# A graph network's edge passes: the right hand side table moves from device memory into on-chip memory

## The reference, cut to what matters

```python
def _gatv2(x, src, dst, edge_attr, Wl, bl, Wr, br, We, att, bo):
    xl = x @ Wl.T + bl
    xr = x @ Wr.T + br
    e = edge_attr @ We.T
    m = xl[src] + xr[dst] + e
    score = jnp.where(m > 0, m, NEG_SLOPE * m) @ att
    smax = jax.ops.segment_max(score, dst, num_segments=N)
    es = jnp.exp(score - smax[dst])
    denom = jax.ops.segment_sum(es, dst, num_segments=N)
    alpha = es / (denom[dst] + 1e-16)
    out = jax.ops.segment_sum(alpha[:, None] * xl[src], dst, num_segments=N)
    return out + bo
h = relu(_gatv2(x, src, dst, edge_attr, Wl1, ...)); h = _instance_norm(h)
h2 = relu(_gatv2(h, src, dst, edge_attr, Wl2, ...) + x @ Wskip.T + bskip)
```

## Time and profile before

| | us |
|---|---|
| median of three timed runs | 7746.43 |
| the profiled execution's own time | 7695.61 |
| its span | 7693.8 |
| PE busy | 5787.1 |
| DVE busy | 4073.2 |
| POOL busy | 3044.5 |
| ACT busy | 2576.5 |

### The profile page before, as it was taken

The page is one execution under the profiler, slowest core; times in us unless marked ns, Lnnn a source line. Parts: engine busy times, 40 slices in busy tenths (PEclk is TensorE's granted clock), DMA queues, the critical chain, the costliest instruction groups (busy, mean ns, idle before and its releaser), DMA issues. The chain is left out here.

```text
span 7693.8 us, 170283 instructions
## 1 busy us (share of the span) xinstructions
PE 5787.1 (75%) x40448; PEld 4192.9 (54%) x40449; DVE 4073.2 (53%) x12741; ACT 2576.5 (33%) x4844; POOL 3044.5 (40%) x3157
## 2 busy tenths in 40 slices
PE   4776777777777776577777777777777697999699
PEld 3555555555555555455555555555555583222689
DVE  6454555555555555455555555554555527778532
ACT  2233333333333333333323333332333215777210
POOL 3455555555555553455555555555555000000000
PEclk9888888888888888788888888888888898999899
DMA  3332322232232222332223323322222372323479
GB/s 78 74 77 67 78 77 71 77 79 69 76 77 68 77 72 60 77 79 69 76 69 78 78 69 77 77 71 77 77 70 77 149 274 78 133 104 109 172 296 362
DMA packets 689322, 764.62 MB, mean 99 GB/s; under 512 B 368995, under 2 KB 574026, under 8 KB 664145
## 3 DMA queue, kind: packets, MB, share of 16 engines
q1 hardware_dynamic: 561703, 577.65, 24.3%
q0 software_dynamic: 100352, 102.96, 6.9%
q10 hardware_dynamic: 27180, 82.93, 2.8%
HBM read 671.04 MB, written 88.81 MB: 99 GB/s over the span
## 5 line engine op out<-in xcount | busy, mean ns | idle before, releaser
L336 POOL DMA_INDIRECT gat_rows<-rows_scr,gat_idx x3136 | 3017.7, 962 | 2881.3 <-PE gat_aps L1352 1261.8
L1343 PE MATMUL gat_tps<-ident,gat_weights 128*128 128x128 f32 x3136 | 602.2, 323 | 1356.4 <-ACTq L1208 1237.9
L1343 PEld LDWEIGHTS gat_tps<-ident,gat_weights 128*128 128x128 f32 x3136 | 384.7, 159 | 1544.8 <-ACTq L1208 1372.0
L1225 ACT ACTIVATE adj_tiles<-gat_counts 128x392 f32 (+1 forms) x784 | 390.6, 498 | 2206.4 <-remote 1153.7
L1361 PE MATMUL gat_sps<-gat_relu,gat_att 128*128 128x256 f32 x3136 | 1084.7, 479 | 0.0
L1124 DVE CUSTOM_DVE_ANT_0 gat_masked<-gat_sps,gat_miss,gat_oldtop 128x512 f32<-128x512 f32 x784 | 586.6, 748 | 782.2 <-remote 513.0
L1075 DVE TENSOR_SCALAR adj_hot_key<-adj_iota_key,adj_winbase,adj_key 128x392 bf16<-128x392 int16 x2416 | 962.1, 398 | 7.6 <-issue 7.6
L1352 PE MATMUL gat_aps<-gat_rows,gat_weightsT 128*128 128x65 f32 x6224 | 957.9, 307 | 0.0
L1352 PEld LDWEIGHTS gat_aps<-gat_rows,gat_weightsT 128*128 128x128 f32 x6224 | 940.8, 231 | 0.0
L1116 DVE COPY gat_oldtop<-gat_top 128x1 f32 x784 | 119.8, 153 | 1354.8 <-issue 610.3
L1074 DVE TENSOR_SCALAR adj_hot_lo<-adj_iota_lo,adj_low 128x128 bf16<-128x128 int16 x2416 | 631.8, 261 | 265.3 <-issue 110.8
(11 more groups left out here) (384 smaller groups left out, 6824.3 us busy)
## 6 DMA issues: line engine op xcount, KB each, us to landing
gcn_sum_adj<-adj_scr SPq DMA_DIRECT2D x98, 1568.0 KB, 8.4
gat_dstb<-dst_scr SPq DMA_DIRECT2D x784, 128.0 KB
gat_ea<-in_ea SPq DMA_DIRECT2D x784, 128.0 KB
gin_sum_adj<-adj_scr SPq DMA_DIRECT2D x49, 1568.0 KB, 8.4
adj_scr<-adj_tiles ACTq DMA_DIRECT2D x48, 1568.0 KB
at_adj<-adj_scr SPq DMA_DIRECT2D x60, 1024.0 KB, 9.5
gat_rows<-rows_scr,gat_idx POOLq DMA_INDIRECT x3136
gat_xr<-xr_scr SPq DMA_DIRECT2D x1568, 24.0 KB
```

Source lines behind the costliest of these rows:

```text
L336: pool.indirect_dma_start(ring.rows[:, u, c, 0:ROW], None, rows_d, bass.IndirectOffsetOnAxis(ap=ring.idx[:, u, c:c + 1], axis=0)).then_inc ...
L1343: last = pe.transpose(tps[:, c * P:(c + 1) * P], wts[:, j, c * P:(c + 1) * P], ident[:])
```

## The change

The table of xr gets a buffer of its own on chip (`plan.right`), with a zeroed column block behind it for the empty row. It is no longer stored. In each visit DVE copies the two halves (64 partitions by 192 columns each) into a small buffer of four slots, from which PE reads as before. The source indices ride as four more 32-bit words at the end of each partition's 256 attribute words, so that one load brings both. To make room, the prologue's search uses other buffers' memory, and the weights and masked scores lie in a node table that is free during the passes; in pass 2 DVE therefore waits until ACT's six copies of the table are done before it clears one of them.

```diff
+RECORD = GE // 2 + GC
...
-def first_indices(sp, tag, words, ring, src_d):
+def first_edges(sp, tag, words, ring, edges_d):
...
-        sp.dma_start(ring.idx[:, u, :], src_d[bass.ds(group_of(sp, pair, group, u), 1), :, :]).then_inc(ring.s_first, 16)
+        sp.dma_start(ring.edges[:, u, :], edges_d[bass.ds(group_of(sp, pair, group, u), 1), :, :]).then_inc(ring.s_first, 16)
...
 def right_table(plan):
-    return plan.tiles[:].rearrange("p s h w d -> p (s h w d)")[:, 0:NT * XR].rearrange("p (t f) -> p t f", f=XR)
+    return plan.right[:, 0:NT, :]
...
-            act.wait_ge(s_part, 6)
-            act.wait_ge(s_clear, 1)
-            store_right(act, xr_d, xr3, empty_row, s_xr_out, [(0, NT)])
             act.wait_ge(s_skip_row, 1)
...
-        xr = sb("xr", [P, RING, XR], BF16)
+        xr = sb("xr", [P, 4, XR], BF16)
...
             def group_parts(u, first=False):
                 g = group_of(sp, pair, group, u)
                 if not first:
-                    sp.dma_start(idx[:, u, :], src_d[bass.ds(g, 1), :, :]).then_inc(s_id[u], 16)
+                    sp.dma_start(edges[:, u, :], edges_d[bass.ds(g, 1), :, :]).then_inc(s_id[u], 16)
                 sp.dma_start(dstb[:, u, :], dst16_d[bass.ds(g, 1), :].to_broadcast([P, GE])).then_inc(s_id[u], 16)
-                sp.dma_start(ea[:, u, :], ea_d[bass.ds(g, 1), :, :]).then_inc(s_ld[u], 16)
-
-            def range_parts(u):
...
-                for j in range(2):
-                    sp.dma_start(xr[HALF * j:HALF * (j + 1), u, :],
-                                 xr_d[bass.ds(blocks[j], 1), :, :]).then_inc(s_ld[u], 16)
...
-            if second:
-                sp.wait_ge(s_clear, 1)
-                store_right(sp, xr_d, xr3, empty_row, s_xr_out, PARTS, s_part)
-                sp.wait_ge(s_xr_out, 80)
-                for u in range(RING):
-                    load_pair(0, u)
-                    range_parts(u)
...
             dve.memset(relu[:, 1, :], 0.0)
+            if second:
+                dve.wait_ge(s_part, 6)
             dve.memset(wtsT[:, 1, :], 0.0)
...
+                    dve.reg_add(blocks[0], fresh[u], 1)
+                    dve.reg_alu(blocks[0], blocks[0], 1, ALU.logical_shift_right)
+                    dve.reg_alu(blocks[1], fresh[u], 1, ALU.logical_shift_right)
+
                     dve.wait_ge(s["top"], count("top", step, 3))
                     dve.wait_ge(s_loaded, step + 1)
                     dve.nop(nofuse=True)
                     dve.tensor_copy(top[:, bass.ds(tb, 1)], newtop[:, (u - 3) % 2:(u - 3) % 2 + 1]).then_inc(s["topped"], 1)
+                    for j in range(2):
+                        part = slice(HALF * j, HALF * (j + 1))
+                        of = dve.snap(blocks[j], min_val=0, max_val=NT)
+                        dve.tensor_copy(xr[part, u % 4, :], plan.right[part, bass.ds(of, 1), :].rearrange("p a f -> p (a f)"))
                     dve.tensor_scalar(hit[:, u % 4, :], near, node, None, ALU.is_equal)
...
-                    pe.wait_ge(s_ld[v], filled * 48 + 48)
                     pe.wait_ge(s_g[v], filled * (16 * GC) + 16 * GC)
                     pe.nop(nofuse=True)
-                    pe.matmul(mps[j][:, 0:GE // 2], we[:], ea[:, v, :], start=True, stop=False)
+                    pe.matmul(mps[j][:, 0:GE // 2], we[:], edges[:, v, 0:GE // 2], start=True, stop=False)
```

More of the change, by code:

```diff
@@ L195, in linear @@
 @phase
-def linear(nc, k, tag, h, w_d, width, out, ident, ring=None, rows_d=None, src_d=None, code_d=None):
+def linear(nc, k, tag, h, w_d, width, out, ident, ring=None, rows_d=None, edges_d=None, code_d=None):
     s_w, s_one = k.sem(tag + "_w"), k.sem(tag + "_one")
@@ L288, in __init__ @@
         self.tiles = sb("tiles", [P, 2, NT, WT, WD], BF16)
+        self.right = sb("right", [P, NT + 1, XR], BF16)
 class Ring:
@@ L371, in prologue @@
     s_skip_w, s_skip_row, s_skip_evac = k.sem("pro_skip_w"), k.sem("pro_skip_row"), k.sem("pro_skip_evacuated")
-    s_part, s_rest, s_xr_out, s_clear = (k.sem("pro_" + n) for n in ("part", "rest", "xr_stored", "empty_row"))
+    s_part, s_rest = (k.sem("pro_" + n) for n in ("part", "rest"))
     xr3, rest = right_table(plan), square
@@ L783, in window_search @@
         def window_search(dve, a):
-            dve.tensor_scalar(junk[:], ranges[:, 1, 0:NCH], wlo[:, a:a + 1], None, ALU.is_ge)
+            dve.tensor_scalar(junk, ranges[:, 1, 0:NCH], wlo[:, a:a + 1], None, ALU.is_ge)
             dve.drain()
-            dve.scalar_tensor_tensor(cond[:], ranges[:, 0, 0:NCH], whi[:, a:a + 1], junk[:], ALU.is_le, ALU.mult)
+            dve.scalar_tensor_tensor(cond, ranges[:, 0, 0:NCH], whi[:, a:a + 1], junk, ALU.is_le, ALU.mult)
             dve.drain()
-            dve.tensor_tensor_reduce(junk[:], cond[:], down[:], 1.0, 0.0, ALU.mult, ALU.max, accum_out=first[:, a:a + 1])
+            dve.tensor_tensor_reduce(junk, cond, down[:], 1.0, 0.0, ALU.mult, ALU.max, accum_out=first[:, a:a + 1])
             dve.drain()
-            dve.tensor_tensor_reduce(junk[:], cond[:], up[:], 1.0, 0.0, ALU.mult, ALU.max, accum_out=last[:, a:a + 1])
+            dve.tensor_tensor_reduce(junk, cond, up, 1.0, 0.0, ALU.mult, ALU.max, accum_out=last[:, a:a + 1])
             dve.drain()
@@ L829, in _ @@
             dve.memset(ring.rows[:, :, :, D:D + 1], 1.0)
-            dve.memset(empty_row[:], 0.0).then_inc(s_clear, 1)
+            dve.memset(plan.right[:, NT, :], 0.0)
             dve.memset(zero[:], 0.0)
@@ L868, in gat_edges @@
     s_loaded = k.sem(tag + "_loaded")
-    s_ld = [k.sem(f"{tag}_in{j}") for j in range(RING)]
-    s_g, s_id, rows, idx = ring.s_g, ring.s_id, ring.rows, ring.idx
+    s_g, s_id, rows, edges = ring.s_g, ring.s_id, ring.rows, ring.edges
     s_hot = [k.sem(f"{tag}_hot_{x}") for x in ("first", "even", "odd")]
@@ L895, in gat_edges @@
         dstb = sb("dstb", [P, RING, GE], I16)
-        ea = sb("ea", [P, RING, GE // 2])
         hit = sb("hit", [P, 4, GE], BF16)
         miss = sb("miss", [P, 4, GE], BF16)
-        xr = sb("xr", [P, RING, XR], BF16)
+        xr = sb("xr", [P, 4, XR], BF16)
         relu = sb("relu", [P, 2, GE // 2])
-        masked = sb("masked", [P, 2, GE])
-        wts = sb("weights", [P, 2, GE])
-        wtsT = sb("weightsT", [P, 2, GE])
+        three = rest[:].rearrange("p t f -> p (t f)")[:, 0:6 * GE].rearrange("p (n j e) -> p n j e", n=3, j=2)
+        masked, wts, wtsT = (three[:, n] for n in range(3))
         newtop = sb("newtop", [P, 2])
@@ L927, in _ @@
             pair = sp.alloc_register(tag + "_sp_pair")
-            half = [sp.alloc_register(f"{tag}_half{j}") for j in range(2)]
             tails = sp.value_load(turns_sb[0:1, 0:1], min_val=1, max_val=(VTAB - TAIL) // TURN)
@@ L1064, in _ @@
             pair = dve.alloc_register(tag + "_dve_pair")
+            blocks = [dve.alloc_register(f"{tag}_block{j}") for j in range(2)]
             for r in carry:
@@ L2477, in lay_out @@
     o = {"x": a["x"], "dst_row": dst}
-    o["src_g"] = src.reshape(NG, GC, P).transpose(0, 2, 1)
     o["src_c"] = src.reshape(EP // P, P).T
     o["dst_c"] = dst.reshape(EP // P, P).T
-    o["ea"] = ea.reshape(NG, 2, GE // 2, D).transpose(0, 1, 3, 2).reshape(NG, P, GE // 2)
+    o["edges"] = np.concatenate([ea.reshape(NG, 2, GE // 2, D).transpose(0, 1, 3, 2).reshape(NG, P, GE // 2),
+                                 src.reshape(NG, GC, P).transpose(0, 2, 1).copy().view(np.float32)], 2)
     for n in (1, 2):
```

72 lines of the change are left out of this document (24 added, 48 removed).

## The result

| | before | after |
|---|---|---|
| median of five timed runs, us | 7745.95 | 7690.55 |
| lowest and highest | 7723.7 to 7751.26 | 7656.6 to 7691.85 |
| ratio, 95% interval | | 0.9926 (0.99 to 0.9951) |
| span of the profiled execution | 7693.8 | 7688.7 |
| DVE busy | 4073.2 | 4468.5 |

The kernel became faster by 0.74%, 55 us, where I had forecast 346 us. The two profiled spans differ by 5 us only: the profiled execution of before lay 28 us under the quickest of its timed runs.

A forecast was written before the change was run, and what follows sets the result against it. PE's updates, late until POOL's gather run ends, were taken to bound the passes. Terms -400 + 80 - 15 - 9 = -344 us gave 7352 on the profiled execution, 7400 us on the timed scale; own range 7250 to 7600 (44%), overall 7130 to 7870.

The forecast's parts named there:

- The loop: Edge passes: PE's updates come late until POOL's gather run ends; cycle is run (5.0 us) plus 1.5 to 2 of chain.
- SP's loads: Edge passes: dropping two table loads a visit relieves the delay by 0.51 us a visit, -400 us, bounds zero or worse to 651.
- the four intervals: Gaps between POOL's last run starts at both passes' ends, SP having nothing left to load: mean 6.81 us against 7.32.
- The sign that I named: If right, mid-pass intervals between POOL's run starts near 6.8 us; also POOL's idle before L336 down some 400 us.
- DVE's copies: Between DVE's hot columns and comparison: two copies plus register work, 0.6 us a visit, one visit in six paying, +80 us.
- First rival: L1061 to L1109: gathers alone make the delay and DVE's work comes on top; 7800 to 7900 us, say 7840; 21%.
- More joined runs: Edge passes: delay starts later, 100 more runs of eight gathers, +330 us, 8130 with DVE's cost; 9%.
- Gather's speed: POOL's gathers stay at about 962 ns, the copies costing nothing; a locked port would give 7714 us, 5%.
- Pass 2: Start of pass 2: no table store and reload, so PE's 45.56 us wait shrinks; -15 us, bounds 0 and 45.
- Prologue: Before the passes: ACT no longer stores the table, where it idled 13.14 us; -9 us counted.
- Scale: Timed runs' median lies 51 us above the profiled execution, so 7352 becomes 7402, stated as 7400 us.

The follow-up runs named there:

- e6: The changed kernel with two of four gathers a visit left out, PE reading old rows for the other half: 5836.42 us, 0.7601 of the kernel before.
- e3b: The changed kernel without any load by SP after the ring is first filled, old edges used over and over: 7653.26 us, 0.996 of the kernel before.
- e1b: The changed kernel without DVE's two copies and their register operations, right hand side left out, PE reading zeros: 7620.65 us, 0.9924 of the kernel before.
- e2c: The kernel before with all its loads plus two further DVE copies a visit into an unread spare buffer: 7668.54 us, 0.9978, before at 7685.79 us.
- e2: The kernel before with all its loads plus two further DVE copies a visit into an unread spare buffer: ratio 1.0014, before at 5904.85 us.
- e2b: Repeat of e2, the kernel before with two further DVE copies a visit: ratio 1.0015, before at 5909.43 us.
- e7: The changed kernel with four separate gathers a visit, behind the sum, scores, counting products and next message: 7122.65 us, 0.9273 of the kernel before.
- e9: The kernel before, with table loads and without DVE's copies, its four gathers spread as in e7: ratio 1.0003, before at 5909.43 us.
- e8: e7 plus a forced POOL pause, four memsets with drains, between second and third gather: 8109.21 us, 1.3733 of the kernel before at 5909.43 us.

## Why the prediction was wrong

- **The loop.** Read rightly: POOL's run of gathers, PE's updates late behind it, the rest hidden. e6 shows it. That some condition beside the gathers is needed, the trace of before could not show.
- **SP's loads, -400 us.** The step that failed. I took "the mean of the four intervals, 0.51 us a visit", against the mean over all visits. The four were all single runs, the 7.32 contained the joined ones; like against like it was 6.81 against 6.89. So the rows gave no reason for a relief of more than some 0.08 us a visit, 63 us. What the runs showed in its place: e3b (0.996) without any load by SP and e1b (0.9924) without table loads and copies gain 31 and 58 us of 7682, some 12 us of it in the prologue. The lower end of my own bounds (zero, "the prologue's rows speak for that") was nearly right.
- **The sign that I named.** "Near 6.8 us" in the middle of a pass came true, 6.82, and meant nothing, since it had been 6.89 before. The sign that could decide was POOL's idle before its gathers: forecast down by some 400 us, it went from 2881.3 to 2876.6.
- **DVE's copies, +80 us.** Their own time came out a little above my 2 x 0.19 us (223 ns each, 0.45 us together); of the 0.2 us for register work no row tells. On the path they were priced wrongly: e2c measures -17 us (-32 to -2), e2 and e2b in the short condition +8 and +9 us. DVE's waits for late updates before L1124 shrank in e2c by half of what the copies took. PE's wait for DVE rose from 41.4 to 140.7 us, above my 110, without lengthening the loop; 22.1 us of it are the first message of pass 2, which no longer waits for the reload.
- **First rival (7840).** Its first half is right, the gathers make the delay without SP's loads; its second half, that DVE's work comes on top, is not.
- **More joined runs.** 114 in the one trace of before became 131, 137 and 141 in three traces of the changed kernel. So this rival came partly true: at my 3.1 to 3.3 us each some 50 to 90 us, against single intervals that became 0.07 to 0.18 us shorter (30 to 75 us). By these counts the two nearly cancel.
- **Gather's speed, 0.** Right: 963 against 962 ns with 350 us more of copies between on-chip buffers. In the trace of after the 582 gathers that overlap a copy take 965 ns in the mean, the others of the passes 955. The lock that the Trainium skill describes (SBUF — State Buffer, "DVE blocks DMA"), by which GpSimd can't write descriptors while such a copy runs, would add up to a copy's 223 ns. The 10 ns measured are far from that, though no trace tells whether these copies ran in a two-port mode.
- **Pass 2, -15 us.** Not resolved. From DVE's first to its last comparison of the pass (L1108, then L1077) it went from 2871.2 to 2862.9 us, -8; in the other two traces of the changed kernel it is 2862.7 and 2838.2. The seam before it stayed at 100.8 us.
- **Prologue, -9 us.** -11.8 us (175.80 to 164.02), the largest part that is certain. ACT's wait for the stores is gone, DVE's wait at its end is 12.8 instead of 25.4 us.
- **Scale.** I added 51 us from the profiled span to the medians; this moved both sides alike and is no part of the miss.

Of the 55, 43 and 43 us between the medians of the three comparisons 12 us are thus placed. The rest, at most 0.06 us a visit, no pair of traces resolves: pass 1 is 17 and 25 us longer in two traces of the changed kernel and 14 us shorter in the third. What of it is shorter intervals and what scatter stays open, and so does what sets the condition in which updates are late.

## What to carry to other kernels

An interval taken from a special place as a stand-in for a future kernel must be compared with intervals of its own kind: sort the ordinary ones first (single and joined runs here), then subtract. When a delay is put down to contention, ask which party could be taken away whole; here SP could be silenced for 0.4%, while POOL's run could be broken, for 7%. Cutting a long burst of one engine's issues so that each piece waits for a later update of the bottleneck's chain (e7, 7122.65 us, the whole computation) cost nothing where the bursts do no harm (the same spread on the kernel before, e9, 1.0003).

## What the runs showed of the hardware

- The same program took 5905 and 7682 us on the same chip in two comparisons. The difference is all in stages where POOL gathers; from ACT's last fifth of the message to the end it took 1684 to 1705 us in all twenty traces. The granted clock over the whole run was 0.96 to 0.97 in the one and 0.87 in the other, but 0.96 again in e6, beside the 7682 us: it follows the work.
- In the long condition, while POOL gathers, SP's two dynamic table loads take 2.24 us from first to last, in the short one 1.17.
- In e8 the operation behind POOL's first memset and drain started 1.62 us later, and the other waits between the gathers cost nothing: four gathers ran 1.25 us apart from pause to pause.
- By the counts of runs in one trace each, less work on SP and DVE went with more joined runs (e1b 142, e3b 155, against 131 to 141), more work on DVE with fewer (e2c 90, before 114).
